# Rounding through int32 instead of adding and subtracting a large constant, in a transformer layer with a ternary-weight FFN

## The reference

```python
def _quant_weight(w):
    s = jnp.clip(jnp.mean(jnp.abs(w)), EPS, None)
    wq = jnp.clip(jnp.round(w / s), -1.0, 1.0) * s
    return w + jax.lax.stop_gradient(wq - w)
def _quant_act(x):
    scale = 127.0 / jnp.clip(jnp.max(jnp.abs(x), axis=-1, keepdims=True), EPS, None)
    xq = jnp.clip(jnp.round(x * scale), -128.0, 127.0) / scale
    return x + jax.lax.stop_gradient(xq - x)
def _bitlinear(x, w):
    return jnp.einsum('bsi,oi->bso', _quant_act(x), _quant_weight(w))
...
def _L0_ffn_ref(x, w1, w2):
    h = jax.nn.gelu(_bitlinear(x, w1), approximate=False)
    return _bitlinear(h, w2)
...
x = x + _L0_attn_ref(_layernorm(x, axis=-1), ...)
x = x + _L0_ffn_ref(_layernorm(x, axis=-1), L0_ffn_w1, L0_ffn_w2)
```

## Time and profile before

| What | us |
|---|---|
| median of 2 runs | 8503.61 |
| lowest and highest | 8487.59, 8519.63 |
| the profiled execution | 8514.42 |
| span of its slowest core, core 0 | 8512.9 |
| spans of the 8 cores | 8458.5 to 8512.9 |
| TensorE, VectorE, ScalarE busy in it | 4176.9, 2201.0, 1927.4 |

### The profile page before, as it was taken

One profiled execution on the slowest core, in us unless ns is written; L12 is line 12 of the kernel. 1 busy time (PEld: TensorE's weight loads), 2 busy tenths in 40 slices (PEclk: granted clock), 3 DMA queues, 4 the chain that ended last, 5 costly groups with the idle time before them and its releaser, 6 DMA issues.

```text
span 8512.9 us, 57707 instructions; the slowest of 8 cores (8458.5 to 8512.9 us)
## 1 busy us (share of the span) xinstructions
PE 4176.9 (49%) x19332; PEld 1642.4 (19%) x19456; DVE 2201.0 (26%) x3953; ACT 1927.4 (23%) x2129; POOL 0.2 (0%) x4
## 2 busy tenths in 40 slices
PE   3315365666666543656666665303333543035545
PEld 0000121222222211212222222101121222012222
DVE  0341423111111114231111111165443444720000
ACT  1112210344444322103444443211110011001111
POOL 0000000000000000000000000000000000000000
PEclk8667675555555556755555555556666676568778
DMA  4233100000000011000000000112112221221221
GB/s 159 101 119 106 40 0 0 1 1 1 1 1 1 23 50 47 0 0 1 1 1 1 1 1 23 62 47 67 59 60 82 83 72 60 82 79 53 66 79 57
DMA packets 199052, 358.57 MB, mean 42 GB/s; under 512 B 23257, under 2 KB 154718, under 8 KB 194674
## 3 DMA queue, kind: packets, MB, share of 16 engines
q1 hardware_dynamic: 198770, 354.87, 12.8%
HBM read 279.29 MB, written 75.50 MB: 42 GB/s over the span
## 4 chain that ended last, share of the span: by engine, by line
PE 43%; DVE 22%; ACT 16%; issue 8%; DMA 6%; SPq 4%; DVEq 1%; ACTq 0%
ACT pslab L763 7%; PE ps_PV L773 6%; PE ps_S L752 6%; PE ps_F L1178 6%; PE ps_F L1066 5%; PE pss L264 4%; PE ps_qn L730 3%; PE ps_W L830 2%; PE ps_mu L606 2%; DVE colmisc L1097 2%; DMA f2xst<-scr_x 2%; DVE ao_tm L785 2%; PE ps_rs L610 2%; PE ps_trH L1117 2%; PE ps_proj L485 1%
## 5 line engine op out<-in xcount | busy, mean ns | idle before, releaser
L752 PE MATMUL ps_S<-qt,kt 65*128 65x512 bf16 x2048 | 984.6, 611 | 279.2 <-ACT pslab L763 242.9
L763 ACT ACTIVATE pslab<-ps_S 128x1024 bf16<-128x1024 f32 x1024 | 994.5, 1021 | 152.3 <-PE ps_S L752 150.5
L773 PE MATMUL ps_PV<-vaug,pslab 128*128 128x65 bf16 x8192 | 531.4, 242 | 457.3 <-DVE ao_tm L785 369.5
L1178 PE MATMUL ps_F<-hqin,w2tb 128*128 128x512 bf16 x2002 | 484.1, 400 | 543.0 <-DMA f2xst<-scr_x 540.2
L783 DVE RECIPROCAL colmisc<-ps_PV 128x1 f32<-128x1 f32 x512 | 86.3, 169 | 1950.3 <-PE ps_PV L773 1950.3
L773 PEld LDWEIGHTS ps_PV<-vaug,pslab 128*128 128x128 bf16 x8192 | 463.3, 129 | 572.9 <-issue 572.9
L264 PE MATMUL pss<-wab,s_onescolf 128*1 128x512 f32 x512 | 309.1, 753 | 534.9 <-ACT wab L244 315.1
L1066 PE MATMUL ps_F<-w1tb,yi_fm 128*128 128x512 bf16 x2000 | 459.8, 390 | 183.4 <-DMA w1tb<-scr_w1t 180.9
L1117 PE MATMUL ps_trH<-s_idb,hqtm 128*128 128x128 bf16 x1024 | 129.5, 306 | 619.7 <-DVE hqtm L1109 518.0
L752 PEld LDWEIGHTS ps_S<-qt,kt 65*128 65x128 bf16 x2048 | 152.4, 108 | 1108.9 <-issue 1108.9
L1178 PEld LDWEIGHTS ps_F<-hqin,w2tb 128*128 128x128 bf16 x2048 | 209.8, 103 | 797.0 <-issue 589.9
(11 more groups left out here) (171 smaller groups left out, 3872.8 us busy)
## 6 DMA issues: line engine op xcount, KB each, us to landing
w1tb<-scr_w1t SPq DMA_DIRECT2D x512, 128.0 KB, 2.5
wst<-w1t SPq DMA_DIRECT2D x24, 2048.0 KB, 9.0
wst<-w2t SPq DMA_DIRECT2D x96, 512.0 KB, 3.5
xstage<-x SPq DMA_DIRECT2D x64, 512.0 KB, 3.6
scr_hq<-hqfm SPq DMA_DIRECT2D x256, 128.0 KB, 2.0
hqin<-scr_hq SPq DMA_DIRECT2D x256, 128.0 KB
scr_x<-x2asm SPq DMA_DIRECT2D x32, 512.0 KB, 2.9
f_xst<-scr_x SPq DMA_DIRECT2D x32, 512.0 KB, 3.2
```

The source lines that it names most:

```text
L752: ins = q.matmul(out=psS[kt % 2][:, 512 * s:512 * (s + 1)], lhsT=kt65[:, N * g + 128 * kt: N * g + 128 * (kt + 1)], rhs=qt65[hb][:, 1024 * ...
L763: sA.inc(q.activation(out=pslab[:, 1024 * kt:1024 * (kt + 1)], in_=psS[kt % 2][:], func=AF.Exp))
L773: ins = q.matmul(out=psPV[:], lhsT=pslab[:, 1024 * kc + 128 * qt: 1024 * kc + 128 * (qt + 1)], rhs=vaug[:, 1040 * g + 65 * kc: 1040 * g + ...
L1178: ins = q.matmul(out=psF[:, half:half + 512], lhsT=w2tb[:, 1024 * hc + 128 * dc: 1024 * hc + 128 * (dc + 1)], rhs=hqin[:, 512 * hc:512 * ( ...
```

## The change

Rounding is done by a copy to an int32 tensor and a copy back. In `w_tern` lines 350 and 352 become such copies over the whole width (through the new `wint`), and the last instruction does both clips. In stage 3 the scaling keeps its place without the addition, and two copies through `yint` (128x1024) follow. In FFN1 the scaling likewise; then the 4096 columns are copied in four pieces of 1024, each out to `hint` (128x1024 int32) and from there to `hqtm` in bf16, every copy waiting for the one before; the count for which TensorE waits is raised by a new one-column copy. Elsewhere the counts and waits are as before.

```diff
@@ w_tern
+        wint = st.enter_context(nc.sbuf_tensor(_u("wint"), [128, cols], I32))
...
-                VS(q, q.tensor_scalar(out=wtmp[:], in0=wtmp[:], scalar1=1.0, scalar2=MAGIC,
-                                      op0=OP.mult, op1=OP.add))
-                VS(q, q.tensor_scalar(out=wtmp[:], in0=wtmp[:], scalar1=MAGIC, scalar2=1.0,
-                                      op0=OP.subtract, op1=OP.min))
-                sV.inc(q.tensor_scalar(out=dst, in0=wtmp[:], scalar1=-1.0, scalar2=None,
-                                       op0=OP.max))
+                VS(q, q.tensor_copy(out=wint[:], in_=wtmp[:]))
+                VS(q, q.tensor_copy(out=wtmp[:], in_=wint[:]))
+                sV.inc(q.tensor_scalar(out=dst, in0=wtmp[:], scalar1=1.0, scalar2=-1.0,
+                                       op0=OP.min, op1=OP.max))
@@ ln3_quant_phase
+        yint = st.enter_context(nc.sbuf_tensor(_u("f_yint"), [128, D], I32))
...
                 VS(q, q.tensor_scalar(out=ytmp[:], in0=ytmp[:], scalar1=colmisc[:, 7:8],
-                                      scalar2=MAGIC, op0=OP.mult, op1=OP.add))
-                sV.inc(q.tensor_scalar(out=yib[:, D * (t % 2):D * (t % 2 + 1)], in0=ytmp[:],
-                                       scalar1=MAGIC, scalar2=None, op0=OP.subtract))
+                                      scalar2=None, op0=OP.mult))
+                VS(q, q.tensor_copy(out=yint[:], in_=ytmp[:]))
+                sV.inc(q.tensor_copy(out=yib[:, D * (t % 2):D * (t % 2 + 1)], in_=yint[:]))
@@ ffn1_phase
+        hint = st.enter_context(nc.sbuf_tensor(_u("hint"), [128, 1024], I32))
...
                     VS(q, q.tensor_scalar(out=ht, in0=ht, scalar1=colmisc[:, 7:8],
-                                          scalar2=MAGIC, op0=OP.mult, op1=OP.add))
-                    sV.inc(q.tensor_scalar(out=hqtm[:], in0=ht, scalar1=MAGIC,
-                                           scalar2=None, op0=OP.subtract))
+                                          scalar2=None, op0=OP.mult))
+                    for sl in range(4):
+                        VS(q, q.tensor_copy(out=hint[:], in_=ht[:, 1024 * sl:1024 * (sl + 1)]))
+                        VS(q, q.tensor_copy(out=hqtm[:, 1024 * sl:1024 * (sl + 1)], in_=hint[:]))
+                    sV.inc(q.tensor_copy(out=colmisc[:, 15:16], in_=colmisc[:, 7:8]))
```

More of the change, by code:

```diff
@@ L10 @@
 F32 = mybir.dt.float32
+I32 = mybir.dt.int32
 BF16 = mybir.dt.bfloat16
```

## The result

The changed kernel takes 8678.04 us (median of 11 runs, 8663.62 to 8691.4), the kernel before 8501.36 us (median of 10 runs). The ratio is 1.0201, with a 95% interval of 1.0183 to 1.022. The ratio is that of the means, which lie 171.3 us apart; the medians lie 176.7 us apart, 2.08%. The forecast was 8666 us and 1.9% slower, with a sum of the steps of 161.9 us, and the interval holds its ratio of 1.0190. The mark of 2% lies inside the interval too.

A forecast was written before the change was run, and what follows sets the result against it. Hand-overs between engines were taken to bound the kernel, with VectorE's tile chain exposed. 0 + 25.6 + 136.3 = 161.9 us on the median 8503.61 gave 8666 us, 1.9% slower; likeliest case 8636 to 8694, range on to 8788.

The forecast's parts named there:

- sum of the steps: Whole kernel: ternarizations 0, third LayerNorm 25.6 and FFN1 136.3 us added make 161.9 us.
- The mark of 2%: Whole kernel: about what a measurement can tell from no change, 170.1 us or 8673.7 us; chance of staying within, about 0.63.
- The unknown price: All three changed places: a cast to or from int32 takes 694 ns at 128x1024, the double rate; chance 0.83.
- single rate: Rival, all three places: int32 casts take 1220 ns at 1024 columns; 398.0 us more, 8902 us; chance 0.08 for both directions.
- fast end: Rival, all three places: 1024-column casts take 427 ns; near 43 us in all, 8546 us; chance 0.03 together with hidden work.
- The ternarizations at 0: Ternarizing w1 and w2: three instructions become three of the same length, so 0 us.
- The third LayerNorm at 25.6 us: Third LayerNorm: one more VectorE instruction per tile, exposed before the transposes; 32 x 0.80 = 25.6 us.
- FFN1 at 136.3 us: FFN1: eight casts and a one-column copy replace one subtraction, 4.26 us a tile, 32 tiles, all exposed; 136.3 us.
- The two waits: FFN1: TensorE's wait for the rounding rises from 518 to some 654 us, ScalarE's for the eviction from 443.9 to some 546.
- The length of a piece: FFN1 and LayerNorm: trace durations used, 694 ns a cast; the skill's 594 ns would make the whole change near 136 us.
- rival 3: Whole kernel: the added work is hidden and the time stays 8504 us; chance 0.03 together with faster casts.
- rival 4: FFN1's matmul bursts: the granted clock moves between 0.82 and 0.87, 27 us at most either way, 8639 to 8693 us.

The follow-up runs named there:

- only_tern: Only the w1 and w2 ternarizations have the new rounding, all else as in the kernel before; 8508.36 us, ratio 0.9998.
- after: The changed kernel itself, with the whole change made to the kernel before; 8678.04 us, ratio 1.0201.
- only_ln3: Only the third LayerNorm has the new rounding, all else as in the kernel before; 8528.15 us, ratio 1.0036.
- wide: The changed kernel, but each FFN1 tile is cast in place and back in one piece, without the one-column copy; 8606.0 us, ratio 1.0124 to the kernel before.
- pieces512: The changed kernel with eight FFN1 pieces of 512 columns instead of four of 1024; 8741.56 us, ratio 1.0276 to the kernel before.
- only_ffn1: Only FFN1 has the new rounding, all else as in the kernel before; 8660.06 us, ratio 1.0188; run again, 8651.5 us, ratio 1.0166.

## Why the prediction was right

**The unknown price.** The casts with int32 were put at 694 ns by the nearest rows, with 1220 and 427 as ends, and took 694 in both directions at 1024 columns, and 2294 at 4096, on the line of the fp32 rows. This was the step on which the rivals of the single rate and the fast end hung; both are refuted by the groups. The rule of two ports in the Trainium skill, "Vector Engine (DVE) Microarchitecture Reference", section 5.1, names no type; the rows with int32 now bear it out.

**The ternarizations at 0.** only_tern shows 0.9998, and no stage of it moved.

**The third LayerNorm at 25.6 us.** 25.2 by the stage in after, 24.8 in only_ln3.

**FFN1 at 136.3 us.** 134.3 in after, and between 130.6 and 137.0 in four profiles. Its tile grew by 4.23 us by the timeline, against 4.26. Two terms were 0.04 us short and cancel: from the start of the last instruction to the transposes it is 2.44 us before, where 2.40 was used, and 0.30 after, where 0.26 was used. The two waits grew to 655.2 and 546.6, within 1.2 us of what was forecast for them.

**The length of a piece.** The estimate by the Trainium skill's "VectorE: DVE Perf Modes", section "The TRN2 errata — SBUF-src ops pay a fixed extra latency per instruction", would have given 136 us for the whole change; the measured gaps of 176.7 and 168.4 us lie above it, and the casts took 694 ns where it gives 594. That section of the Trainium skill says itself that the figure comes out too small for the copy it was held against, and puts the measured fixed term near 150 cycles. At its 0.96 GHz a cast's 694 ns are 666 cycles, 154 more than the half of 1024 columns, so the trace agrees with that term. The direction was borne out by wide and pieces512: cuts cost.

**The work hidden** (rival 3) is refuted by every kernel with the new FFN1 or LayerNorm. **The burst clock** (rival 4) did not move in the two bursts read: 0.87 and 0.82 in both kernels.

**What the sum missed** is 14.8 us of the 176.7 between the medians. No run puts it into the changed places, where the stages grew by 158.7: one profile has 16.6 us in stages of which only the w1 ternarization was touched (and only_tern shows that at nothing), its repeat -1.0, and by the mean core span the repeat lies 161.8 us above before, as the steps say. What remains in the first runs of after and only_ffn1 stays open. The forecast counted on such scatter in its range, but took the chance of staying within 2% at 3 in 4. The ratio came out at 1.0201, with the repeat at 1.0189, and both intervals hold 1.02, so on which side of 2% the change lies is not shown. That the forecast stood 8 us from the mark was known, and the scatter between executions of the attention stages alone (22.7 us) is larger than that.

## What to carry to other kernels

Where the waits show that one engine's sequence holds up all others, count steps, not busy time: each instruction costs its length plus the 0.11 us of its wait, and the change could be summed before it was run: by the mean core span, to within 4 us of 8500 in four of the five runs of it or a part of it, and to 12.6 in the fifth. A type change rides for free on an instruction that is needed anyway (an int32 output of a scaling), while a cast and a cast back are two full passes. Cut an operation into pieces only where each piece releases another engine; otherwise each further instruction costs about 0.27 us here (0.80 for a step, of which 1024 columns at 0.52 ns are 0.53). Leaving out the waits between the pieces takes back most of that and not all: FFN1 took 1537.8 us in four pieces with waits, 1495.0 without, and 1479.7 in one piece.

## What the runs showed of the hardware that was not expected

Two instructions of VectorE with no wait between them overlap even when each is a full-width cast: 0.60 us from start to start for casts of 0.69 us, against 0.80 with a wait. The rows before the change had shown it only behind a one-column instruction (5545.90 to 5545.97 in the earlier trace rows).

Code of the same length took 5489.7 to 5512.4 us up to the end of attention in one execution or another (mean of the 8 cores), and one and the same kernel 5512.4 and 5496.1: differences larger than the whole error of this forecast. Differences of 10 us in this kernel are read from the stage in which the edit lies, not from the total.
